# One head's value products moved to another side group, and a norm check by 128 flags in two columns instead of a transposed row

## The reference

```python
mod = (silu(c) @ wmod).reshape(4, 6, 1, -1)
sa, ca, ga, sb, cb, gb = (mod[:, k] for k in range(6))
ga, gb = (sign of each, with a size of at least 0.25)
h = layernorm(x) * (1 + ca) + sa
qkv = (h @ Wqkv.T + bqkv).reshape(B, 16, S, 24)      # a raw reshape: a head is 64 rows of h
q, k, v = split(qkv, 3, axis=-1)
attn = softmax(q @ k.T / sqrt(8))
x = x + ga * ((attn @ v).reshape(B, S, 128) @ Wo.T + bo)
h = layernorm(x) * (1 + cb) + sb
probs = softmax(h @ router_w.T); topk_vals, topk_idx = top_k(probs, 2)
w = topk_vals / (sum(topk_vals) + 1e-6)
x = x + gb * sum over the two of (h @ expert_weights[idx] + probs[idx]) * w
```

## Time and profile before

| | us |
|---|---|
| median of 3 runs | 556.71 (555.5 to 557.04) |
| the profiled execution | 557.98 |
| its span on the core | 556.1 |
| PE busy | 519.1 |
| ACT busy | 494.8 |
| DVE busy | 362.8 |
| POOL busy | 219.2 |

### The profile page before, as it was taken

How to read it: one execution, slowest core, us unless ns; L and a number is a source line. 1 busy time by engine, 2 the same in 40 slices (tenths; PEclk the granted TensorE clock), 3 DMA queues, 4 the chain that set the end, 5 groups by cost and what they waited for, 6 DMA issues and landing times. The chain is left out here.

```text
span 556.1 us, 14357 instructions
## 1 busy us (share of the span) xinstructions
PE 519.1 (93%) x4064; PEld 215.3 (39%) x4064; DVE 362.8 (65%) x1271; ACT 494.8 (89%) x571; POOL 219.2 (39%) x429
## 2 busy tenths in 40 slices
PE   7488889999999999999999999999999999999983
PEld 6233333334343434343433333343434343433352
DVE  4435457677867666677767667677676666664466
ACT  1279989999999999999999999999999999998962
POOL 1223233344443334444443343444433344443335
PEclk9999999999999999999999999999999999999997
DMA  4573333333333333333333333333333332333010
GB/s 100 128 199 90 89 96 78 77 97 88 89 90 89 96 98 84 76 78 93 88 90 90 98 93 83 72 88 91 88 89 95 98 86 65 91 96 84 17 32 14
DMA packets 85497, 48.44 MB, mean 87 GB/s; under 512 B 61508, under 2 KB 76240, under 8 KB 85456
## 3 DMA queue, kind: packets, MB, share of 16 engines
q1 hardware_dynamic: 70162, 43.07, 30.0%
q10 hardware_dynamic: 15294, 4.82, 3.8%
HBM read 32.91 MB, written 14.94 MB: 86 GB/s over the span
## 5 line engine op out<-in xcount | busy, mean ns | idle before, releaser
L547 ACT ACTIVATE probs<-ps_scores 128x1024 f32<-128x1024 f32 x512 | 485.8, 1028 | 42.9 <-DMA q_scr<-qk_parts 19.6
L735 PE MATMUL ps_attn<-probs,values 128*32 128x512 f32 x2048 | 248.1, 599 | 0.4 <-issue 0.4
L717 PE MATMUL ps_scores<-query_stack,key_stack 32*128 32x512 f32 x1024 | 130.7, 500 | 17.5 <-ACT probs L547 11.4
L717 PEld LDWEIGHTS ps_scores<-query_stack,key_stack 32*128 32x128 f32 x1024 | 49.4, 183 | 167.9 <-ACT probs L547 164.1
L422 POOL TENSOR_SCALAR var_eps<-moments 128x1 f32<-128x1 f32 x64 | 12.3, 192 | 222.7 <-DVE moments L1078 149.5
L735 PEld LDWEIGHTS ps_attn<-probs,values 128*32 128x32 f32 x2048 | 54.0, 109 | 110.5 <-issue 110.3
L765 PE MATMUL ps_side<-experts_gated,h2T 128*128 (+1 forms) x228 | 74.7, 409 | 0.0
L1067 DVE RECIPROCAL sums_inv<-sums 128x128 f32<-128x128 f32 x32 | 30.5, 952 | 32.5 <-DMA attnT<-a_scr 32.5
L1074 DVE TENSOR_TENSOR x<-ps_side,x_gated 128x128 f32<-128x128 f32 x31 | 9.0, 292 | 60.8 <-PE ps_side L765 57.2
L1150 DVE TENSOR_TENSOR weighted<-ps_side,coef 128x256 f32<-128x256 f32 x114 | 46.5, 408 | 2.4 <-PE ps_side L765 2.4
L471 POOL TENSOR_TENSOR mix<-weighted 128x512 f32<-128x512 f32 x31 | 39.7, 1280 | 0.0
(11 more groups left out here) (129 smaller groups left out, 498.9 us busy)
## 6 DMA issues: line engine op xcount, KB each, us to landing
key_stack<-k_scr SPq DMA_DIRECT2D x128, 128.0 KB, 2.7
query_stack<-q_scr SPq DMA_DIRECT2D x121, 64.0 KB, 2.2
q_scr<-qk_parts SPq DMA_DIRECT2D x188, 32.0 KB, 2.0
k_scr<-qk_parts SPq DMA_DIRECT2D x64, 64.0 KB, 1.7
a_scr<-attn ACTq DMA_DIRECT2D x126, 18.0 KB
sums<-a_scr SPq DMA_DIRECT2D x32, 64.0 KB, 2.1
attnT<-a_scr SPq DMA_DIRECT2D x32, 64.0 KB, 2.2
out_dram<-out_all ACTq DMA_DIRECT2D x29, 64.0 KB, 1.8
```

The costliest lines, as they stand in the source:

```text
L547: nc.scalar.activation(probs[:, k % RING, g, :], ps_scores[:, slot(k, g), :], ACT.Exp, scale=SCALE)\
L717: mm = nc.tensor.matmul(out_, key_stack[p0:p0 + 32, parity, 2 * k:2 * k + 2, :].rearrange("p j r -> p (j r)"), query_stack[p0:p0 + 32, par ...
L735: mm = nc.tensor.matmul(ps_attn[q:q + 32, :], values[:, parity, g, k, :], probs[:, k % RING, g, h * HALF:(h + 1) * HALF], start=(k == 0), ...
```

## The change

- The value products of tile t+1 are split by head. From tile 2 on, those of head 0 are issued in group 0, behind the projection, and those of head 1 stay in group 1. The event that DVE waits for comes with head 1's.
- `a_norm_max` on DVE has a second instruction, which turns each partition's maximum into a flag: 1 where it is at most 214.
- The product against the identity (128 columns) becomes one with two columns of ones (`a_flags`): its result is the number of flags, in every partition.
- `a_bounded` on DVE loses its reduce over the row and compares the number in partition 0 with 127.5. PE's group 1 waits for this (`bounded_done`) where it waited for the reduce.
- `ident_r` and the copy that filled it are gone.

```diff
-                nc.tensor.matmul(ps, norm_max[:].broadcast_to([P, P]), ident_r[:], start=True, stop=True).then_inc(ev["normT_done"], 1)
+                reached(pe, ev["norm_flag_done"], u1)
+                nc.tensor.matmul(ps, norm_flag[:].broadcast_to([P, P]), ones[:, 0:2], start=True, stop=True).then_inc(ev["flags_done"], 1)
...
-            def a_project_v(u1, ring, col):
-                for n in range(G):
+            def a_project_v(u1, ring, col, heads=range(G)):
+                for n in heads:
...
-                mm.then_inc(ev["v_ps_done"], 1)
+                if n == G - 1:
+                    mm.then_inc(ev["v_ps_done"], 1)
...
             def side0(ps, at, batch, parity, before, after, past):
                 if past < 2 <= before:
                     c_project(ps, at[-1], batch[2])
+                if before >= 2 and after >= 1:
+                    a_project_v(at[2], 1 - parity, P, (0,))
                 if after >= 1:
-                    a_normT(ps[:, P:2 * P], at[2])
+                    a_flags(ps[:, P + R:P + R + 2], at[2])
                 if past < 4 <= before:
                     c_experts(ps, at[-4], batch[4], parity, 2)

             def drained0(at, before, after, past):
                 if after >= 1:
-                    reached(pe, ev["norm_top_done"], at[2])
+                    reached(pe, ev["bounded_done"], at[2])
...
             def side1(ps, at, batch, parity, before, after, past):
...
                 if before >= 2 and after >= 1:
-                    a_project_v(at[2], 1 - parity, P)
+                    a_project_v(at[2], 1 - parity, P, (1,))
...
             def a_norm_max(ps, n1):
                 v.tensor_reduce(norm_max[:], ps, AX.X, ALU.max).then_inc(ev["norm_max_done"], 1)
+                reached(dve, ev["norm_max_done"], n1)
+                v.tensor_scalar(norm_flag[:], norm_max[:], NORM2_MAX, 1.0, ALU.is_le, ALU.mult).then_inc(ev["norm_flag_done"], 1)
             def a_bounded(src, n1, ring):
-                reached(dve, ev["normT_done"], n1)
-                v.tensor_reduce(norm_top[:], src, AX.X, ALU.max).then_inc(ev["norm_top_done"], 1)
-                reached_apart(dve, ev["norm_top_done"], n1, x_first, 16)
-                v.tensor_scalar(bounded_int[0:1, ring, :], norm_top[:], NORM2_MAX, 1.0, ALU.is_le, ALU.mult)\
-                    .then_inc(ev["bounded_done"], 1)
+                reached_apart(dve, ev["flags_done"], n1, x_first, 16)
+                v.tensor_scalar(bounded_int[0:1, ring, :], src, P - 0.5, 1.0, ALU.is_ge, ALU.mult).then_inc(ev["bounded_done"], 1)
...
-                v.tensor_copy(ident_r[:], ident[:])
```

More of the change, by code:

```diff
@@ L154, in adaln_block @@
         squares = sb("squares", [P, 2, P], F32R)
-        norm_max = sb("norm_max", [P, 1], F32R)
-        ident_r = sb("ident_r", [P, P], F32R)
-        norm_top = sb("norm_top", [1, 1])
+        norm_max = sb("norm_max", [P, 1])
+        norm_flag = sb("norm_flag", [P, 1], F32R)
         bounded_int = sb("bounded_int", [P, 2, 1], I32)
@@ L228, in adaln_block @@
             qkT_done qk_hi_done qk_parts_done values_done
-            squares_done norms_done norm_max_done normT_done norm_top_done bounded_done
+            squares_done norms_done norm_max_done norm_flag_done flags_done bounded_done
             attn_saved sums_inv_done valsT_done attn_proj_done x_gated_done x1_done
@@ L672, in a_norms, with a_flags @@
                 mm.then_inc(ev["norms_done"], 1)
-            def a_normT(ps, u1):
-                reached(pe, ev["norm_max_done"], u1)
-                nc.tensor.matmul(ps, norm_max[:].broadcast_to([P, P]), ident_r[:], start=True, stop=True).then_inc(ev["normT_done"], 1)
+            def a_flags(ps, u1):
+                reached(pe, ev["norm_flag_done"], u1)
+                nc.tensor.matmul(ps, norm_flag[:].broadcast_to([P, P]), ones[:, 0:2], start=True, stop=True).then_inc(ev["flags_done"], 1)
             def exact_maxima(t, parity):
@@ L949, in _ @@
             a_norms(ps_scores[:, 1, 0:2 * J], 1)
-            a_normT(ps_scores[:, 1, HALF:HALF + P], 1)
+            a_flags(ps_scores[:, 1, HALF:HALF + 2], 1)
             a_transpose(2)
@@ L1158, in written0 @@
                 elif after >= 1:
-                    reached(dve, ev["normT_done"], at[2])
+                    reached(dve, ev["flags_done"], at[2])
             def written1(at, before, after, past):
@@ L1208, in tile @@
                 if after >= 1:
-                    a_bounded(banks[0][0:1, P:2 * P], at[2], 1 - parity)
+                    a_bounded(banks[0][0:1, P + R:P + R + 1], at[2], 1 - parity)
                 if past < 2 <= before:
@@ L1331, in prologue @@
                 a_xhat(1, 2)
-                a_bounded(ps_scores[0:1, 1, HALF:HALF + P], 1, 0)
+                a_bounded(ps_scores[0:1, 1, HALF:HALF + 1], 1, 0)
                 a_moments(2, 3)
```

## The result

| | before | changed |
|---|---|---|
| median, us | 557.22 (555.5 to 557.5, 6 runs) | 565.12 (564.26 to 566.35, 6 runs) |
| profiled execution, us | 557.98 | 564.84 |
| span on the core, us | 556.1 | 563.0 |
| ratio | | 1.0146, 95% interval 1.0128 to 1.0164 |

The changed kernel is 7.9 us slower. Forecast were 9.1 us more and 565.8 us.

The account below looks back on a forecast made before the run. Two rings of waits bound it, PE with ACT and group 0 through DVE and POOL to the norms; the latter sets the period. 12 x 0.47, 12 x 0.25 and 3 x 0.16 give +9.1, 565.8 us; range 560.5 to 569.5.

Parts of the forecast that it names:

- D: Group 0 on PE: everything behind the moved value products comes 0.47 us later, from a gap in front and their passes.
- Odd tiles: Loop: PE's attention products release attn, slack of 0.24 us absorbs part, so the DVE and POOL chain carries 0.25 us.
- Even tiles: Loop: x1hat binds attn, no slack, so the chain carries 0.47 us to squares, the norms and the next tile.
- Tiles 28 to 30: Written-out tiles with a shorter chain: ring A decides, 3 x 0.16 = 0.5 us more.
- The check: Two-column product and the reduce removed from DVE: 0 us, since full loads cost 0.11 anyway and x1hat waits for POOL.
- Group 1's gain: Group 1 loses four passes, 0.11 us, of which ACT lets 0.09 through; worth nothing in the loop.
- R1: Rival: odd tiles lose their earlier x1, so every loop tile pays D; 568.5 us, chance 0.13.
- R4: Rival: no gaps around the moved products but their passes paid, D = 0.11; 558.0 us, chance 0.06.
- R2: Rival: the DVE and POOL chain shrinks, only ring A counts, 27 tiles x 0.16; 561.0 us, chance 0.13.
- ring A: PE and ACT: side group, then scores waiting for ACT's exponential; forecast to grow by 0.25 - 0.09 = 0.16 us a tile.
- R3: Rival, faster: value loads slip in without a gap in group 0 and POOL's rstd comes sooner; 554.3 us, chance 0.05.
- R5: Rival, worse: x1hat misses its transpose and the flags' later work reaches the next tile; over 569.5 us, chance 0.07.

Follow-up runs that it names:

- run 3: The changed kernel with head 0's value products at the head of group 0, ahead of the projection: 560.28 us beside 556.20 for the kernel before.
- run 4: The changed kernel with head 0's value products issued twice in group 0: 568.12 us beside 556.20 for the kernel before.
- run 1: The changed kernel with both heads' value products back in group 1, so the norm check by flags alone: 556.64 us beside 556.20 before.
- run 2: The changed kernel with the old check's costs back (64-column flags' product, reduce on DVE): 564.71 us beside 556.20 for the kernel before.
- run 9: The kernel before with both heads' value products first in group 1 and DVE's statistics ahead of x1hat, old norm check kept: 554.15 us beside 557.07.
- run 7: The kernel before with both heads' value products at the head of group 1, ahead of the transpose: 556.50 us beside 556.60.
- run 5: The changed kernel with DVE's statistics of a later tile moved ahead of x1hat: 559.98 us beside 556.60 for the kernel before.
- run 6: The kernel before with DVE's statistics of a later tile moved ahead of x1hat: 555.64 us beside 556.60.
- run 8: The kernel before with the flags check, both heads' value products first in group 1, and DVE's statistics ahead of x1hat: 554.23 us beside 556.60.

## Why the prediction was right, point by point

**D, the delay inside group 0:** forecast 0.47, measured 0.47 (0.46 by the median of the loop's even tiles). Both of its parts were read from places where the same products stood already, the gap in front from tile 1 and the rest from group 1; runs 3 and 4 show the parts apart.

**The scores behind group 0:** 0.25 later, measured 1.43 - 1.18 = 0.25.

**Odd tiles:** forecast 0.25, measured 15.99 - 15.75 = 0.24.

**Even tiles: the term that was mis-sized.** Forecast were 0.47 each, measured are 16.10 - 15.75 = 0.35. The step that failed is "attn at 283.43 with no idle time before it", which I read as a chain without slack. In even tiles too attn was waiting for PE's attention products, with an idle time of zero in the row. These products behind group 0, on PE's timeline, before (tiles 16 and 17):

```profile
281.44 1.92 PE L735 MATMUL ps_attn<-probs,values 128*32 128x512 f32 x16
...
297.19 1.92 PE L735 MATMUL ps_attn<-probs,values 128*32 128x512 f32 x16
```

and in the changed kernel:

```profile
284.85 1.92 PE L735 MATMUL ps_attn<-probs,values 128*32 128x512 f32 x16
...
300.96 1.92 PE L735 MATMUL ps_attn<-probs,values 128*32 128x512 f32 x16
```

Before, they end at 283.36 and 299.11, and attn starts 0.07 us later in both tiles, at 283.43 and 299.18; the row of the odd tile names PE. In the changed kernel's odd tile it is again 0.07 (302.95 - 302.88), but in its even tile 0.20 (286.97 - 286.77), and there attn starts 0.26 us after x1hat's start, before x1hat's recorded end at 287.06. Before, it started 283.43 - 283.09 = 0.34 after x1hat's start. All loop tiles but the first, tile 4, show the same within 0.02. So x1hat could have let attn start 0.08 earlier than it did, and the first 0.08 of an even tile's delay was room. This also corrects the reading that the end of group 0 set the period before: attn then waited in both tiles for products that follow scores which waited for ACT, and the end of group 0 took over only with the change.

From x1 to the end of squares are 295.46 - 284.68 = 10.78 us, 291.94 - 281.05 = 10.89 before. Of these 0.11, attn's room is 0.08 and x1hat comes 0.01 earlier behind x1; the last 0.02 lie behind attn and are near the rounding of the rows.

In odd tiles the room was larger than I read, too: x1hat could let attn start at 298.59 + 0.26 = 298.85 before, 0.33 ahead of its start and not 0.24. So PE binds there with 0.12 us to spare (302.95 against 302.57 + 0.26), not by 0.02.

**Sum over the loop:** 12 x 0.35 + 12 x 0.24 = 7.1 us instead of 8.6. The two traces agree with the per-tile figures:

Weight loads of the projection in tiles 5 and 28, the kernel before:

```profile
106.60 0.19 PEld L744 LDWEIGHTS ps_side<-wo_gated,valsT 128*128 128x128 f32 x1 [0.25 <-issue]
...
468.79 0.30 PEld L744 LDWEIGHTS ps_side<-wo_gated,valsT 128*128 128x128 f32 x2 [0.24 <-issue]
...
517.18 0.30 PEld L744 LDWEIGHTS ps_side<-wo_gated,valsT 128*128 128x128 f32 x2 [0.24 <-issue]
```

and the changed one; the third row of each is tile 31:

```profile
106.53 0.30 PEld L744 LDWEIGHTS ps_side<-wo_gated,valsT 128*128 128x128 f32 x2 [0.24 <-issue]
...
475.51 0.19 PEld L744 LDWEIGHTS ps_side<-wo_gated,valsT 128*128 128x128 f32 x1 [0.24 <-issue]
...
524.11 0.19 PEld L744 LDWEIGHTS ps_side<-wo_gated,valsT 128*128 128x128 f32 x1 [0.24 <-issue]
```

Tiles 5 to 27 take 368.98 us, 362.19 before: 6.8 more for 11 even and 12 odd tiles, and 11 x 0.35 + 12 x 0.24 = 6.7. **Tiles 28 to 30** take 48.60 us, 48.39 before: 0.2 more where I had 0.5. Ahead of tile 5 the profiled executions differ by -0.07, where the forecast had +0.47 from tile 4. Tile 4 by itself did take 0.45 more (106.53 - 90.14 against 106.60 - 90.66), but tile 3 took less: PE's 16 passes of attention products took 2.94 us before and 1.92 in the changed one, after 0.29 of idle time (timelines of PE, before and changed):

```profile
75.63 2.94 PE L735 MATMUL ps_attn<-probs,values 128*32 128x512 f32 x16
```

```profile
76.09 1.92 PE L735 MATMUL ps_attn<-probs,values 128*32 128x512 f32 x16 [0.29 <-issue]
```

What interrupts them there is not named by the profile and was not pursued. The start varies by more than that in any case: the projection of tile 5 starts at 105.24 in run 1, which has no moved products, and at 106.60 in the kernel before. The measured terms add up to 6.8 + 0.2 - 0.1 = 6.9 us, as far as the two profiled spans lie apart, and the medians lie 7.9 apart. So part of the closeness of 7.9 to the forecast 9.1 is luck: by its terms the forecast was 2.2 too high, 1.4 of it in tiles 5 to 27, nearly all in the even ones.

**The check:** 0, as forecast (runs 1, 2 and 9, by the loop within 0.2 us). The wait moved from norm_top_done to bounded_done cost nothing that shows.

**Group 1's gain is worth nothing in the loop:** right, and run 7 shows it for the whole of the 0.09.

**The rivals.** R1 (every loop tile pays D, 568.5) and R4 (no gaps, 558.0) are out by the periods and by runs 3 and 4. R2 (only ring A) would be true of a kernel with a shorter DVE chain, and run 5 is that kernel: 559.98, forecast for R2 were 561.0. R3 needed value loads without a gap; there is one. R5 came near: in the even tile x1hat's transpose loads at 287.17, 0.11 us behind x1hat's recorded end and not the 0.05 that I took from ACT and POOL, so it is 0.03 late (0.28 of idle time in front of it in place of 0.25). That costs nothing, since the norms wait 0.18 for squares later in the same tile. One sign in my list was off: the norms' load comes 0.54 us behind the router's first load, not some 0.4; by my own terms it should have said 0.34 + 0.47 - 0.16 = 0.65.

## What to carry to other kernels

Before work is moved into a gap, count the borders between array shapes that it makes: here a pair of 64-column passes costs 0.06 us among its like, but two pairs set between full products cost 0.47, so they belong beside other shape changes or at a group's edge. Room that an engine has before its own next wait is not room on the path: ask also who else waits for the end of that group, and follow that ring round to where it closes. And where two rings have nearly the same length, shortening one shows little (1.0 us in run 6, 0.1 in run 7); the edit on both (run 8) gives 2.4.

## What the runs showed of the hardware that I had not expected

In the loop DVE's next instruction starts up to 0.09 us before the recorded end of the one ahead (attn at 286.97, x1hat's end at 287.06), so an idle time of zero in a row of DVE can hide a wait of that size. Compare start to start with another execution of the same pair, and look whether the start follows some other engine's end by a fixed time in every tile, as attn's 0.07 us behind PE's products does. And the norm check's product, a single pass, takes 0.11 us from its load to the next between other full products, with 2 columns (run 1), with 64 (run 2: loads at 299.29 and 299.40) and with 128 (before).
